# First product of every expert as three matmuls of rounded parts, in the tiles of the token experts and in the stage of the sequence experts

## What is computed

```
def _ffn(h, w1, b1, w2, b2):
    return jax.nn.gelu(h @ w1 + b1, approximate=False) @ w2 + b2
...
for l in range(L):
    x = x + _attn(_ln(x, ln1_w[l], ln1_b[l]), wq[l], wk[l], ...)
    h = _ln(x, ln2_w[l], ln2_b[l])
    moe = _token_moe if l % 2 == 0 else _seq_moe
    x = x + moe(h, gate_w[l], gate_b[l], e_w1[l], e_b1[l], e_w2[l], e_b2[l])
```

## Time and profile before

| what | value |
| --- | --- |
| median of 3 runs | 1320.65 us (1312.6 to 1324.02) |
| profiled execution: its span, first to last instruction | 1327.3 us |
| PE busy in the span | 1215.2 us (92%) |
| DVE, ACT, POOL busy | 926.7, 803.1, 710.5 us |
| tiles, about | 737 to 930 us |
| last stage, about | 1186 to 1316 us |

### The profile page before, as it was taken

One profiled execution on the slowest core, in us unless ns is written; L12 is line 12 of the kernel. 1 busy time (PEld: TensorE's weight loads), 2 busy tenths in 40 slices (PEclk: granted clock), 3 DMA queues, 4 the chain that ended last, 5 costly groups with the idle time before them and its releaser, 6 DMA issues.

```text
span 1327.3 us, 30592 instructions
## 1 busy us (share of the span) xinstructions
PE 1215.2 (92%) x9884; PEld 990.1 (75%) x9884; DVE 926.7 (70%) x2791; ACT 803.1 (61%) x1629; POOL 710.5 (54%) x1279
## 2 busy tenths in 40 slices
PE   4999999998887699999999899999999999989996
PEld 3777777766665477777777799898677777769996
DVE  6799999988777779989985221125788888635553
ACT  4566666775665366666666556564666666654552
POOL 4455555664231156777778431332677775445654
PEclk9899999998898799999998899999899999979998
DMA  4788776425666354555442787786565565255773
GB/s 118 218 230 239 221 225 185 125 71 155 167 168 163 94 141 127 128 131 136 120 118 63 225 231 232 229 254 209 140 154 146 152 155 148 79 156 166 213 201 103
DMA packets 208291, 216.94 MB, mean 163 GB/s; under 512 B 46403, under 2 KB 157507, under 8 KB 208132
## 3 DMA queue, kind: packets, MB, share of 16 engines
q1 hardware_dynamic: 191088, 193.49, 54.0%
q0 software_dynamic: 6304, 14.43, 3.9%
q10 hardware_dynamic: 10740, 7.06, 1.7%
HBM read 126.90 MB, written 85.46 MB: 160 GB/s over the span
## 4 chain that ended last, share of the span: by engine, by line
PE 66%; DVE 13%; issue 5%; SPq 5%; ACT 4%; DMA 4%; POOL 3%; POOLq 0%; DVEq 0%; ACTq 0%
PE scores L619 6%; PE weights L1573 6%; PE values L709 5%; PE weights L673 5%; PE scores L1831 4%; PE weights L678 4%; PE weights L1847 4%; PE values L716 3%; PE scores L1557 3%; PE scores L628 3%; DVE negmax L1014 3%; SPq L475 3%; DMA windows<-parts 2%; PE tokens L648 2%; PE tokens L582 2%
## 5 line engine op out<-in xcount | busy, mean ns | idle before, releaser
L1170 POOL TENSOR_SCALAR_AFFINE_SELECT probs<-probs 128x256 f32<-128x256 f32 (+1 forms) x576 | 279.5, 490 | 228.7 <-ACT probs L859 225.4
L859 ACT ACTIVATE probs<-weights 128x512 f32<-128x512 f32 x448 | 264.9, 598 | 120.3 <-PE weights L673 86.8
L1014 DVE TENSOR_REDUCE negmax<-scores 128x4 f32<-128x512 f32 x384 | 261.3, 685 | 86.2 <-PE scores L619 83.2
L619 PE MATMUL scores<-keys,queries 128*128 128x512 f32 (+1 forms) x384 | 186.1, 487 | 6.0 <-issue 1.7
L859 ACT ACTIVATE probs<-weights,keybias 128x512 f32<-128x512 f32 x192 | 131.5, 688 | 64.3 <-PE weights L673 48.0
L673 PE MATMUL weights<-queries,keys 104*128 104x256 f32 x768 | 159.0, 290 | 1.0 <-issue 0.6
L673 PEld LDWEIGHTS weights<-queries,keys 104*128 104x128 f32 x768 | 139.9, 194 | 22.3 <-issue 3.6
L1018 DVE TENSOR_REDUCE negmax<-scores 128x2 f32<-128x512 f32 (+1 forms) x192 | 131.0, 686 | 29.2 <-PE scores L625 19.4
L678 PEld LDWEIGHTS weights<-queries,keys 104*128 104x128 f32 x768 | 114.8, 195 | 10.2
L678 PE MATMUL weights<-queries,keys 104*128 104x128 f32 x768 | 110.2, 268 | 0.0
L709 PE MATMUL values<-probs,v 128*32 128x256 f32 x1536 | 106.6, 396 | 3.5 <-POOL probs L1170 3.5
(11 more groups left out here) (285 smaller groups left out, 2747.1 us busy)
## 6 DMA issues: line engine op xcount, KB each, us to landing
windows<-parts SPq DMA_DIRECT2D x192, 192.0 KB
queries<-windows SPq DMA_DIRECT2D x64, 384.0 KB
hidden_room<-in_m_w SPq DMA_DIRECT2D x78, 256.0 KB, 3.1
out_room<-in_m_w SPq DMA_DIRECT2D x78, 256.0 KB, 3.2
keys<-windows SPq DMA_DIRECT2D x192, 96.0 KB
routed_rows<-zeros SPq DMA_DIRECT2D x64, 256.0 KB, 3.6
windows<-parts SPq DMA_DIRECT2D x64, 120.0 KB
expert_rows<-probs ACTq DMA_DIRECT2D x46, 128.0 KB, 3.1
```

Of the source, the lines that this page charges most:

```text
L619: i = pe.matmul(bank[:], queries[0:rows, s, t * P:(t + 1) * P], keys[0:rows, s::S4, half * P:(half + 1) * P], start=True, stop=True)
L859: act.activation(probs[:, n % RING], weight_banks[n % 2][:], ACT.Exp, scale=SCALE, **bias).then_inc(exp_done.sem, 1)
L1014: i = dve.tensor_reduce(most[:, part, s, :], bank[:].rearrange("p (a k) -> p a k", k=P), AX.X, ALU.max, negate=True)
L1170: pool.affine_select(out=block, in_=block, compare_op=ALU.is_ge, fill=0.0, base=0, pattern=[[0, heads], [1, P]], channel_multiplier=-1).th ...
```

## The change

Each float32 product `w1 . src` becomes three float32r matmuls into the same bank: high.high, high.low, low.high, where high is the rounded value and low is the value minus high. The parts have to be made:

- tiles: VectorE rounds and subtracts, both for the rows (128x256) and the weights (128x512) of every tile. The parts lie in two buffers each.
- last stage: ScalarE rounds the weights (two of 128x512 for each sequence), VectorE subtracts them, and VectorE makes both parts of the rows (128x256). They lie in unused rows of the `keys` buffers.

Room for the parts comes from letting buffers of the early stages (`early_room`) share space with buffers of the later ones. Several pieces begin one or two slots earlier; the first weights of the last stage are loaded apart from the others.

```diff
             def pe_hidden(pe, j):
...
-                pe.wait_ge(tile_src_ready.sem, tile_src_ready.at(j))
-                pe.wait_ge(weights_loaded.sem(j), weights_loaded.at(j))
+                high_rows, low_rows_of = keeprows[j % 2][:], low_tokens[j % 2][:]
+                pe.wait_ge(rows_split.sem, rows_split.at(j))
+                pe.wait_ge(weights_split.sem, weights_split.at(j))
...
-                        i = pe.matmul(bank[:, k * T:(k + 1) * T], hidden_w[j % WEIGHTS][:, c * P:(c + 1) * P],
-                                      tile_src[j % LANES], start=True, stop=True)
+                        high, low = (weight_parts[j % 2][:, part, c * P:(c + 1) * P] for part in range(2))
+                        pe.matmul(bank[:, cols], high, high_rows, start=True, stop=False)
+                        pe.matmul(bank[:, cols], high, low_rows_of, start=False, stop=False)
+                        i = pe.matmul(bank[:, cols], low, high_rows, start=False, stop=True)
...
+            def dve_rows(dve, j):
+                high, low, rows = keeprows[j % 2][:], low_tokens[j % 2][:], tile_src[j % LANES]
+                if j >= 2:
+                    dve.wait_ge(hidden_ready.sem, hidden_ready.at(j - 2, 2))
+                dve.wait_ge(tile_src_ready.sem, tile_src_ready.at(j))
+                dve.tensor_copy(high, rows).then_inc(rows_high.sem, 1)
+                yield
+                dve.wait_ge(rows_high.sem, rows_high.at(j))
+                dve.tensor_tensor(low, rows, high.bitcast(F32), ALU.subtract).then_inc(rows_split.sem, 1)
+                yield
+
+            def dve_weights(dve, j):
+                high, low, weights = weight_parts[j % 2][:, 0], weight_parts[j % 2][:, 1], hidden_w[j % WEIGHTS]
+                if j >= 2:
+                    dve.wait_ge(hidden_ready.sem, hidden_ready.at(j - 2, 2))
+                dve.wait_ge(weights_loaded.sem(j), weights_loaded.at(j))
+                dve.tensor_copy(high, weights).then_inc(weights_high.sem, 1)
+                yield
+                dve.wait_ge(weights_high.sem, weights_high.at(j))
+                dve.tensor_tensor(low, weights, high.bitcast(F32), ALU.subtract).then_inc(weights_split.sem, 1)
+                yield
...
-                return slots(pe, (0, 4, pe_hidden), (3, 5, pe_out), (-4, 6, pe_rows))
+                return slots(pe, (0, 4, pe_hidden), (3, 5, pe_out), (-5, 6, pe_rows))
...
-                return slots(act, (0, 3, act_hidden), (-3, -1, act_rows), (6, 5, act_store))
+                return slots(act, (0, 3, act_hidden), (-4, -1, act_rows), (6, 5, act_store))
...
-                return slots(dve, (5, 3, dve_out)) + tables
+                return slots(dve, (5, 3, dve_out), (-2, 5, dve_rows), (-2, 4, dve_weights)) + tables
...
-                return slots(pool, (-9, 3, pool_rows))
+                return slots(pool, (-10, 3, pool_rows))
```

And in the last stage:

```diff
             def pe_hidden(pe, q):
                 lane = q % LANES
-                pe.wait_ge(weights_loaded.sem(q), weights_loaded.at(q))
+                pe.wait_ge(src_split.sem, src_split.at(q))
...
                     e, half = divmod(r, 2)
+                    if half == 0:
+                        pe.wait_ge(weights_split.sem, weights_split.at(q, e + 1))
                     for k in range(2):
...
+            def act_weights(act, q):
+                lane = q % LANES
+                parts_free(act, q)
+                act.wait_ge(first_loaded.sem(q), first_loaded.at(q))
+                for e in range(K2):
+                    act.copy(w_parts[lane][:, 0, e], hidden_w[lane][:, e]).then_inc(weights_high.sem, 1)
+                    yield
+
+            def dve_weights(dve, q):
+                lane = q % LANES
+                for e in range(K2):
+                    dve.wait_ge(weights_high.sem, weights_high.at(q, e + 1))
+                    dve.tensor_tensor(w_parts[lane][:, 1, e], hidden_w[lane][:, e], w_parts[lane][:, 0, e].bitcast(F32),
+                                      ALU.subtract).then_inc(weights_split.sem, 1)
+                    yield
+
+            def dve_src(dve, q):
+                lane = q % LANES
+                parts_free(dve, q)
+                dve.wait_ge(src_ready.sem, src_ready.at(q))
+                dve.tensor_copy(src_parts[lane][:, 0], srcT[lane][:]).then_inc(src_high.sem, 1)
+                yield
+                dve.wait_ge(src_high.sem, src_high.at(q))
+                dve.tensor_tensor(src_parts[lane][:, 1], srcT[lane][:], src_parts[lane][:, 0].bitcast(F32),
+                                  ALU.subtract).then_inc(src_split.sem, 1)
+                yield
...
-                yield
+                yield from rest(3 if q >= LANES else 1)
                 dve.wait_ge(spread_ready.sem, spread_ready.at(q))
...
             def sp_stages(sp):
-                return slots(sp, (-18, 4, sp_fetch, True), (-5, 3, sp_weights, True), (-1, 4, sp_base, False), (12, 5, sp_store, False))
+                return slots(sp, (-20, 4, sp_fetch, True), (-7, 3, sp_weights, True), (-1, 4, sp_base, False), (12, 5, sp_store, False))
 
             def pe_stages(pe):
-                return slots(pe, (0, 4, pe_hidden, False), (3, 5, pe_out, False), (-8, 6, pe_gate, True))
+                return slots(pe, (0, 4, pe_hidden, False), (3, 5, pe_out, False), (-10, 6, pe_gate, True))
 
             def act_stages(act):
-                return slots(act, (0, 3, act_hidden, False), (-8, 4, act_gate, True))
+                return slots(act, (0, 3, act_hidden, False), (-10, 4, act_gate, True), (-3, 5, act_weights, False))
 
             def dve_stages(dve):
-                return slots(dve, (4, 3, dve_out, False), (-12, 4, dve_gate, True))
+                return slots(dve, (4, 3, dve_out, False), (-14, 4, dve_gate, True), (-4, 5, dve_src, False), (-2, 5, dve_weights, False))
 
             def pool_stages(pool):
-                return slots(pool, (-11, 2, pool_first, True), (8, 1, pool_last, False), (0, 3, pool_base, False))
+                return slots(pool, (-13, 2, pool_first, True), (8, 1, pool_last, False), (0, 3, pool_base, False))
```

More of the change, by code:

```diff
@@ L233, in decoder @@
             w[n] = const(n, [P, 1])
-        for n in ("a_gamma", "a_beta"):
-            w[n] = const(n, [P, C])
         for n in w:
@@ L296, in decoder @@
         hsum = [const(f"hsum{k}", [P, 1]) for k in range(2)]
-        base_sum = [const(f"base{k}", [P, NT, C]) for k in range(2)]
+        base_sum = routed
         pool_step = semaphore("pool_step")
@@ L1828, in pe_hidden @@
                     e, half = divmod(r, 2)
+                    if half == 0:
+                        pe.wait_ge(weights_split.sem, weights_split.at(q, e + 1))
                     for k in range(2):
-                        c = 2 * half + k
-                        i = pe.matmul(hidden_banks[n % 3][:, k * T:(k + 1) * T], hidden_w[lane][:, e, c * P:(c + 1) * P], srcT[lane][:],
-                                      start=True, stop=True)
+                        into, chunk = hidden_banks[n % 3][:, k * T:(k + 1) * T], slice((2 * half + k) * P, (2 * half + k + 1) * P)
+                        high, low = (w_parts[lane][:, part, e, chunk] for part in range(2))
+                        pe.matmul(into, high, src_parts[lane][:, 0], start=True, stop=False)
+                        pe.matmul(into, high, src_parts[lane][:, 1], start=False, stop=False)
+                        i = pe.matmul(into, low, src_parts[lane][:, 0], start=False, stop=True)
                     i.then_inc(hidden_ready.sem, 1)
@@ L1882, in act_hidden, with parts_free @@
                     yield
+            def parts_free(engine, q):
+                if q < LANES:
+                    before = last - 2 + q
+                    engine.wait_ge(st_ready.sem, st_ready.at(before, units[before].n))
+                else:
+                    engine.wait_ge(hidden_ready.sem, hidden_ready.at(q - LANES, 2 * K2))
+            def act_weights(act, q):
[17 more added lines that the diff above has]
+                dve.tensor_copy(src_parts[lane][:, 0], srcT[lane][:]).then_inc(src_high.sem, 1)
+                yield
+                dve.wait_ge(src_high.sem, src_high.at(q))
+                dve.tensor_tensor(src_parts[lane][:, 1], srcT[lane][:], src_parts[lane][:, 0].bitcast(F32),
+                                  ALU.subtract).then_inc(src_split.sem, 1)
+                yield
             def norm_stats(dve, which, z):
```

44 lines of the change are left out of this document (31 added, 13 removed).

## The result

The changed kernel took 1354.6 us (median of 4 runs, 1353.5 to 1355.8), the kernel before 1317.8 beside it (1312.6 to 1324.0): ratio 1.0269, 95% interval 1.0228 to 1.0309, slower by 36.8 us. Forecast: 1342, range 1306 to 1360. The profiled execution took 1353.5 us, span 1351.9.

What follows compares the result with a forecast made beforehand. TensorE was taken as the bound, busy for 92% of the span. Tiles -6, round trip net of products +15.5 and clock +12 gave +21.5 us on the median 1320.65, so 1342 us, range 1306 to 1360.

Steps and rivals of the forecast that it cites:

- The price of the products: Tiles and last stage: three float32r matmuls at 0.12 us each save 0.073 us a product, 22.9 us in all.
- The far row of 0.155: Dearer float32r matmuls, 0.155 us each for 256 columns; as a rival 33 us more, 1375 us, chance 0.03.
- The round trip: Last stage: logits, VectorE's chain, subtraction, first product; TensorE idle 1.95 us in most sequences, 24.9 us together.
- The rival without a round trip: Last stage: no such wait, so it gains its 9.4 us; whole kernel -15, 1305 us; chance 0.15.
- The clock: Last stage: TensorE's clock falls to 0.89 because of the idle pieces, 13 x 0.92 = 12 us.
- The tiles: Tiles stage: products -13.5, gather +4.1, clock stretch +1.7, end phase +2, net -6 us.
- gather: Tiles: VectorE's wait for the first gather now stops TensorE at the start of slot 56, costing 4.1 us.
- clock stretch: Tiles: one more stretch at half clock behind the idle time at the first gather, 1.7 us.
- end phase: Last 12 slots of the tiles: VectorE also reduces scores and prepares units, 2 us, between 0 and 5.
- late weights: Tiles: weights wanted two slots earlier, out of a lead of seven; charged nothing, up to 4 us kept for the range.
- rival of the bound tiles: Tiles: VectorE or DMA becomes the bound and the tiles gain nothing; 21.5 + 10, 1352 us, chance 0.07.

Runs made afterwards that it cites:

- order_sp: `order`, with SyncE also keeping the two expert numbers it has read instead of reading them again: 1323.1 us, ratio 1.0003 to the kernel before.
- order: Changed kernel with VectorE's last-stage weights subtraction moved ahead of the gate's chunk in the same slot: 1337.8 us, ratio 1.010 to the kernel before.
- last_only: Only the last stage changed, tiles as in the kernel before: 1350.9 us, ratio 1.0216 to the kernel before.
- ahead4: Changed kernel with the first three sequences' gates and other run-ahead work, weight loads too, 4 slots early instead of 6: 1344.9 us, ratio 1.0167.
- after_again: The changed kernel, unedited, measured and profiled once more: 1355.9 us, ratio 1.0269 to the kernel before.
- tiles_rank: Kernel before with only the tiles changed, VectorE's roundings of rows and weights at earlier ranks 1.6 and 1.5: 1311.6 us, ratio 0.993.

## Why the prediction was right, and where it was off

**The price of the products: right.** 0.12 us for a pass, in every group of three. The clean proof is `order_sp`: beats of 7.43 us, the 8.02 of before less 8 x 0.073 = 0.59. The far row of 0.155 is out. By the rule of the Trainium skill (FP8 and Floating Point Precision, section TensorE Precision Notes) that true FP32 takes four passes, from which the prediction estimates 0.108 us less a product, that beat would have been 8.02 - 8 x 0.108 = 7.16; the beats of 7.43 speak against that estimate here.

**The round trip: right, its size 5% over.** Before sequences 2 to 12 TensorE idles 1.83 us, before 13 1.45, and before 1 2.20 (there a last step of attention stands between, L739): 23.8 in all, where the sum had 24.9. Moving the one subtraction removed them. The rival without a round trip is what `order` built, and even then SyncE stood in the way: that rival would not have given its 9.4 us.

**The clock: right in kind, its size met in one execution and too large for the other.** Forecast 12 us, spread over all beats. What happens is a stretch of 3.4 us at half level behind about every other idle piece: six of them, 1.56 us each, 9.4 us, and one of 5.8 us behind the first, longer piece, which costs half of that, 2.9, together 12.3. The second execution had five, without the long one, 7.8 us: 4.5 less, and its last stage was 4.8 shorter. The last stage as a whole: forecast 157, measured 155.6 and 150.8, and 150.6 to 154.6 in four variants with the same round trip.

**The tiles: the term that failed is the weights.** The sum had -6: products -13.5, gather +4.1, a clock stretch +1.7, end phase +2. The gather's idle was 6.61 instead of 2.22, +4.4. The clock stretch behind it is some 3 us and was there before too, so its 1.7 was charged for nothing. But the late weights, at which I charged nothing and held 4 us for the range, cost 2.6 to 5.0 us idle and in most executions 1.6 more at half clock. Smaller idle pieces that the kernel before doesn't have come on top: 0.80 and 0.75 before L756, 0.43 and 0.82 before L1563. In all, TensorE idles 14.1 us in the stage of the profiled execution where it had idled 4.6. With the 1.6 at half clock the -13.5 become -2.4, and the stage shows -1.9. The tiles measured 190.3 and 191.9 in two executions of the changed kernel, up to 195.6 in variants with the same tiles, against 192.1 (and 189.0 in `last_only`): on the whole no gain. The end phase can't be told apart from this. In the recorded rival of the bound tiles the sum adds 10 us where its words, no gain at all, ask for 13.5; the range stays the same.

**Not in the sum: the transition.** 4.7 us against the profiled execution before, 2.5 against the other. The gates and weight loads of the first sequences moved two slots up into the attention. I had listed the slots and priced only the waits. `ahead4` shows 6 to 7 us, all executions together 2 to 7.

**The baseline.** The stages add up to 24.6 us between the two profiled spans (tiles -1.9, transition +4.7, last stage +25.7, rest -3.9). The medians differ by 36.8. The forecast of +21.5 comes near the first number and misses the second by 15. That it comes so near the first is partly luck: the transition and the rest, neither of them in the sum, nearly cancel. Of the 12.2 us between the two numbers, 11.1 are that the profiled execution of the kernel before (about 1328.9 us, its span and the 1.6 us that the others have over theirs) was that much over its median, and 1.1 that the changed kernel's was under its own. The second profiled execution before (1326.6 us) was long too, in runs that go from 1312.6 to 1332 us. The 36.8 themselves are no accident: `after_again`, beside 13 runs of the kernel before, has 36.5. I added the sum to the median, as if the profiled stalls were the median's; the 6.7 us between them were 0.5% in my text and should have been in the range as they stand. Which stretch makes the short executions of the kernel before short stays open: none was profiled. Over all kernels the time to the first scores of the decoder layers is 429 to 435 us and from there to the tiles 298 to 306; and code of the kernel before took 189.0 us for the tiles in `last_only` and 23.9 for the transition in `tiles_rank`, 3 and 2 us under its own profile.

## What to carry to other kernels

When work moves from a deep pipeline's background (VectorE, with slack) to just before TensorE's next instruction, read the whole in-order queue ahead of it: one wait for TensorE's own last result makes a round trip, and it cost 1.83 us a sequence here, though VectorE was busy for only 58 of 100 us. Price an idle piece with the half-clock stretch that may follow, and expect the next bound right behind it: here a second read of a number on SyncE, unnoticed until the first bound was gone. A change that measures 2.7% slower can hold a gain of 0.9% that four small edits set free.

## What the runs showed of the hardware

- Idle pieces of the same 1.83 us were followed by the half level about every other time and not in between (windows at 1227.1 and 1238.0: 0.53 and 1.00). Beats of 9.31 and 10.87 us mix in all six executions with this round trip, at most two of a kind in a row. With the piece filled by matmuls the clock was 1.00 for 80 us. It was 1.00 too from 1260 to 1300 us of `order`, where TensorE was busy for only 34.31 of 40 us but no idle piece was longer than 1.07.
- The half level behind one such piece lasts 3.4 us; in the transition of the changed kernel it lasted nearly 24 us, with TensorE busy for 22.58 of 24.
- Reading a number from memory into SyncE's registers costs about 0.65 us of its queue, beside 0.33 to 0.43 us for most DMA issues (single ones up to 1.85). Twelve issues and four reads filled 8.7 us, twelve issues and two reads 7.23 at best and 7.99 in the mean of eight.
- One wait of VectorE for the same transfer (6.3 to 8.7 us) cost TensorE 0.7 to 2.2 us in one queue order, 6.0 to 6.7 in another and 2.7 to 3.7 in a third.
